# Edge weights and one-hot numbers read from PSUM in a graph attention kernel

## The chip, the cores and the metric

One core of one Trainium2 chip. The metric is the time of one execution in microseconds of device time; lower is better. The core has five engines that run beside each other: TensorE (PE in the profile), VectorE (DVE), ScalarE (ACT), GpSimd (POOL) and SyncE (SP), which here only issues transfers. They tell each other through semaphores what is done.

## What is computed

A layer norm with ReLU, and two graph attention layers with four heads of 64 channels over 12,500 nodes and 200,000 edges that are sorted by their destination, plus a self loop for each node. Cut to what matters:

```python
def _gat_layer(h_in, W, a_s, a_d, b, src, dst, n):
    h = (h_in @ W).reshape(n, Hh, Cc)
    alpha_s = jnp.sum(h * a_s, axis=-1)
    alpha_d = jnp.sum(h * a_d, axis=-1)
    e = jax.nn.leaky_relu(alpha_s[src] + alpha_d[dst], 0.2)
    m = jax.lax.stop_gradient(jax.ops.segment_max(e, dst, num_segments=n))
    ex = jnp.exp(e - m[dst])
    alpha = ex / jax.ops.segment_sum(ex, dst, num_segments=n)[dst]
    out = jax.ops.segment_sum(h[src] * alpha[:, :, None], dst, num_segments=n)
    return out.reshape(n, Hh * Cc) + b

h = jnp.maximum(_layernorm(x), 0.0)
h = gelu(_gat_layer(h, W0, a_src0, a_dst0, b0, src, dst, n))
h = gelu(_gat_layer(h, W1, a_src1, a_dst1, b1, src, dst, n))
return x + h
```

## The kernel before

A prelude of some 200 us norms the nodes, multiplies them by W0 and stores for each node a row of 264 float32 numbers in a table in DRAM: for each of four heads 64 channels and the two logits. Then each layer is a loop over 112 steps. A step takes a chunk of 1792 edges (14 slots of 128 partitions) and a window of 128 destination nodes. For it,

- SP loads the edges' fields (`edge`, line 354), a broadcast row of destinations (`dst_b`, line 359), marks (`mark`, line 363) and the window's own rows (`self_row`, line 377). These loads are issued in this order, each behind a wait for its buffer. The load of `self_row` waits for `own_part` of four steps back, and the next step's `edge` load stands behind it in SP's order.
- POOL gathers the source rows of the edges with 14 indirect DMAs of 128 rows each (line 495) into `rows_all[u]`, one of four buffers. The group of 14 waits for the sum of four steps back and for the edge fields to land.
- DVE builds one-hots that map edges to nodes (`onehotT`, line 838, from 16-bit numbers; `onehot`, line 883, float32, 1792 elements for each partition), finds the maximum along each run of edges of one destination by scans (lines 875, 877 within a partition; 897, 899 across partitions, after PE has transposed the ends of the partitions, lines 1110 and 1111), gets the carries back through PE (lines 1117, 1118) and reads them in line 957 (`reach`), and ends with `fall`, the logit minus its maximum (line 973).
- ACT takes the exponential (line 593) and writes it straight into column 64 of each head of the gathered rows in SBUF.
- In the next body DVE multiplies the rows of slots 0 to 9 by that column in three products (line 861, parts of 4, 3 and 3 slots, so 1024, 768 and 768 elements), after a small product in line 858; ACT multiplies slots 10 to 13 with 16 small instructions (line 566). PE sums all rows by node with the one-hots (line 1128), in four parts.
- Then follow the shares of the window's own node and of the sum handed over from the window before, the mean, Gelu, and either the row for the next layer's table or the residual.

A body of the loop works on four steps at once: `after` (the newest: one-hots, scans, exponential), `now` (weighing and summing), `before` (shares and means) and `earlier` (next layer's row or residual). The loops are unrolled by four bodies. Each engine runs through its own list in a fixed order. For the DVE it is, in `dve_body`: one-hots of nodes and logits (after), product part 0 (now), residual (earlier), copy of the gathered logits to `value` (`take_values`, line 867, which waits for all 14 gathers), product part 1, the scans, product part 2, the one-hot of edges, `run_max` (line 890), scans across partitions (after), shares (before), logits and falls (after), means (before). For PE, in `pe_body`: logits to edges (line 1101), sum part 0, transposes of the ends (lines 1110, 1111), part 1, next row, part 2, carries back (1117, 1118), part 3, hand over (1138).

PSUM banks: 0 logits of edges, 1 ends of runs, 2 carries, 3 and 4 sums, 5 hand over, 6 and 7 the next layer's row. The functions that the change touches:

## Time and profile before

| | us |
|---|---|
| median of three runs | 5451.78 |
| lowest and highest | 5431.81, 5456.39 |
| the profiled execution, its own time | 5461.54 |
| its span, first to last instruction | 5459.7 |
| DVE busy | 3275.1 |
| POOL busy | 3349.7 |

The profile is of one execution. A busy time is the sum of an engine's instruction times; a line of the costliest groups gives an engine, an operation, what it writes and reads with its size, how often, the busy time and the mean of one in ns, and behind the second bar the idle time of the engine just before it and what ended most of that. "issue" there is time for which the profile shows no releaser; "remote" is an event of another engine that can't be named. A semaphore's message can come later than the end of the instruction that sent it. The ends of matmuls are modelled.

### The profile page before, as it was taken

To read this page: it belongs to the slowest core of one execution; us is meant where nothing else is said; L and a number is where in the kernel's file an instruction comes from. 1 tells how busy PE (TensorE), PEld (TensorE's weight loads), DVE (VectorE), ACT (ScalarE), POOL (GpSimd) and SP (SyncE) were. 2 spreads that over 40 slices of the span, in tenths; PEclk is the share of its full clock that TensorE was granted. 3 is DMA by queue.
4 is the path that set the end of the run, shared out by engine and by line. 5 is a ranking of instruction groups with operands and counts; after the bars stand their busy time and mean duration, and the time that the engine had idled before them with its cause. 6 is when DMAs were issued, how large, how long until landed. Compare 5 with 4: busy or idle time off the path is not lost. (4 is left out here: it accounts for less than half of the span.)

```text
span 5459.7 us, 66711 instructions
## 1 busy us (share of the span) xinstructions
PE 2814.1 (52%) x12030; PEld 2001.2 (37%) x12030; DVE 3275.1 (60%) x12165; ACT 2232.4 (41%) x6943; POOL 3349.7 (61%) x3188
## 2 busy tenths in 40 slices
PE   6454555555545555555544545455545545454544
PEld 5333433333433433333333333333333333332333
DVE  5465666555756665656645656666666655665665
ACT  4243444444434443444433334344433434343434
POOL 2466666666666666666646656666656666566563
PEclk9777777777777777767766777767767777776777
DMA  6444444444444443444434444444444444444443
GB/s 209 122 114 112 119 118 116 117 116 118 118 119 111 120 116 111 113 114 119 118 88 120 120 118 131 126 125 131 127 125 131 126 125 132 123 130 123 123 128 85
DMA packets 342321, 662.86 MB, mean 121 GB/s; under 512 B 99106, under 2 KB 211530, under 8 KB 341914
## 3 DMA queue, kind: packets, MB, share of 16 engines
q0 software_dynamic: 151056, 429.17, 29.8%
q1 hardware_dynamic: 128952, 172.16, 10.6%
q10 hardware_dynamic: 62018, 59.05, 3.2%
q14 instruction: 286, 2.34, 0.1%
q8 instruction: 9, 0.15, 0.0%
HBM read 597.44 MB, written 62.65 MB: 121 GB/s over the span
## 5 line engine op out<-in xcount | busy, mean ns | idle before, releaser
L495 POOL DMA_INDIRECT rows_all<-table,edge x3136 | 3309.3, 1055 | 2042.6 <-issue 1430.9
L1128 PE MATMUL bank<-rows_all,onehot 128*128 128x264 f32 x6272 | 2144.3, 500 | 199.8 <-remote 99.9
L1128 PEld LDWEIGHTS bank<-rows_all,onehot 128*128 128x128 f32 x6272 | 1513.7, 252 | 569.1 <-issue 244.1
L566 ACT ACTIVATE rows_all<-rows_all 128x64 f32<-128x64 f32 x3584 | 877.2, 333 | 10.3 <-issue 6.8
L1101 PE MATMUL bank<-logit_p,onehotT 128*128 128x24 bf16 x3136 | 118.7, 180 | 1209.8 <-issue 875.7
L861 DVE TENSOR_TENSOR rows_all<-rows_all 128x768 f32<-128x768 f32 (+1 forms) x672 | 695.1, 1035 | 0.0
L1101 PEld LDWEIGHTS bank<-logit_p,onehotT 128*128 128x128 bf16 x3136 | 101.4, 103 | 1315.3 <-issue 1160.8
L897 DVE TENSOR_TENSOR_SCAN runs<-mark,runs,bank 4x128 f32<-4x128 f32 x224 | 104.8, 468 | 733.2 <-issue 635.3
L579 ACT ACTIVATE share<-node_d 128x8 f32<-128x8 f32 x224 | 46.7, 209 | 1162.1 <-DVE node_d L944 809.8
L602 ACT ACT_TABLE_LOAD x224 | 287.4, 1283 | 567.7 <-issue 409.5
L883 DVE TENSOR_TENSOR onehot<-iota_f,dloc 128x1792 f32<-128x1792 f32 x224 | 453.7, 2026 | 1.8 <-remote 0.9
L1138 PE MATMUL bank<-total,heir 128*128 128x264 f32 x448 | 182.8, 496 | 489.0 <-DVE heir L979 251.6
L579 ACT ACT_TABLE_LOAD x222 | 284.8, 1283 | 163.3 <-issue 160.6
L574 ACT ACTIVATE act_oT<-bank 128x256 f32<-128x256 f32 x112 | 42.5, 379 | 643.8 <-remote 531.3
L1138 PEld LDWEIGHTS bank<-total,heir 128*128 128x128 f32 x448 | 79.2, 221 | 591.4 <-DVE total L978 333.1
L593 ACT ACTIVATE rows_all<-fall 128x56 f32<-128x56 f32 x224 | 67.8, 303 | 511.3 <-DVE fall L973 315.7
L957 DVE TENSOR_TENSOR reach<-edge,bank 128x112 f32<-128x112 f32 x224 | 59.8, 267 | 339.5 <-remote 300.6
L1117 PE MATMUL bank<-ident,carry 4*128 4x4 f32 x224 | 49.3, 220 | 397.1 <-DVE carry L904 310.3
L588 ACT ACTIVATE own_part<-self_row,share 128x64 f32<-128x64 f32 x896 | 239.2, 357 | 0.0
L1154 PE MATMUL bank<-w_ext,act_oT 128*128 128x264 f32 x448 | 138.4, 437 | 171.3 <-issue 121.7
L584 ACT ACTIVATE old_part<-bank,share 128x65 f32<-128x65 f32 x896 | 208.2, 316 | 9.6
L1117 PEld LDWEIGHTS bank<-ident,carry 4*128 4x128 f32 x224 | 32.5, 145 | 482.2 <-issue 482.2
(163 smaller groups left out, 3545.5 us busy)
## 6 DMA issues: line engine op xcount, KB each, us to landing
dst_b<-dst_row SPq DMA_DIRECT2D x224, 448.0 KB
rows_all<-table,edge POOLq DMA_INDIRECT x3136
self_row<-table SPq DMA_DIRECT2D x224, 132.0 KB
table<-row ACTq DMA_DIRECT2D x113, 132.0 KB
x_row<-in_x_dram SPq DMA_DIRECT2D x112, 128.0 KB
out_dram<-y_out ACTq DMA_DIRECT2D x112, 128.0 KB
act_pad<-act_o ACTq DMA_DIRECT2D x112, 128.0 KB
table<-row ACTq DMA_DIRECT2D x24, 528.0 KB, 3.8
```

The lines of the kernel that those rows point to most:

```text
L495: nc.gpsimd.indirect_dma_start(out=G[u][:, j, :], out_offset=None, in_=table[L][0:N, :], in_offset=bass.IndirectOffsetOnAxis(ap=index[:, j ...
L566: last = nc.scalar.activation(G4[t.u][:, j, h, 0:C], G4[t.u][:, j, h, 0:C], ACT.Copy, scale=G4[t.u][:, j, h, C:C + 1])
L579: nc.scalar.activation(share[:], node_d[:], ACT.Exp).then_inc(s["share_ready"], 1)
L584: last = nc.scalar.activation(old_part[:, h, :], bank[5][:, h * HW:h * HW + C + 1], ACT.Copy, scale=share[:, 1, h:h + 1])
L588: last = nc.scalar.activation(own_part[:, h, :], self_row[t.u][:, h * HW:h * HW + C], ACT.Copy, scale=share[:, 0, h:h + 1])
L602: nc.scalar.activation(act_o[t.half][:], mean_o[:], ACT.Gelu).then_inc(s["act_ready"], 1)
L861: nc.vector.tensor_tensor(rows[:, :, 0:C], rows[:, :, 0:C], rows[:, :, C:C + 1].broadcast_to([P, (t1 - t0) * H, C]), ALU.mult).then_inc(s[ ...
L883: nc.vector.tensor_tensor(onehot[t.half][:], wide(iota_f[:], 1, SLOTS), wide(dloc[:], 2, P), ALU.is_equal).then_inc(s["onehot_ready"], 1)
L1101: last = nc.tensor.matmul(bank[0][:, j * w:(j + 1) * w], onehotT[t.half][:, j, :], logit_p[:].rearrange("d q k h -> d (q k h)"), start=Tru ...
L1128: last = nc.tensor.matmul(bank[3 + t.half][:, 0:ROW], onehot[t.half][:, j, :], G[t.u][:, j, :], start=(j == 0), stop=(j == SLOTS - 1))
L1138: nc.tensor.matmul(bank[5][:, 0:ROW], heir[:], total[:].rearrange("p h c -> p (h c)"), start=True, stop=True).then_inc(s["old_done"], 1)
L1154: last = nc.tensor.matmul(bank[7][:, 0:ROW], act_oT[:, j, :], w_ext[:, 1, j, :], start=(j == 0), stop=(j == KC - 1))
```

## The change

Three things:

1. The exponentials of an edge chunk are written to PSUM (`edge_w`, bank 2) and then copied from there by ACT into the rows' column in SBUF. The DVE's three products and the small product in front of them take the weight from `edge_w`; ACT's own products and PE's sum still use the column.
2. The numbers 0 to 127 with which the one-hot of edges is compared lie in PSUM (`numbers`, bank 1) instead of in SBUF (`iota_f`). The carries move from bank 2 to bank 1 (`carries`). As PE and DVE now both use bank 1, PE's transposes of the ends also wait for the one-hot of the same step and for `reach` of the step before.
3. The one-hot of edges goes from behind the third product to a place in front of `take_values`, which waits for the gathered rows.

```diff
+        numbers = bank[1][:, 2 * P:3 * P]
+        carries = bank[1][:, 3 * P:3 * P + 2 * H]
+        edge_w = bank[2][:, 0:SLOTS * H]
...
             def weigh_last(t):
-                act.wait_ge(s["w_ready"], t.done(0))
+                act.wait_ge(s["wcol_ready"], t.done(0))
...
             def exponentials(t):
                 act.wait_ge(s["fall_ready"], t.done(0))
-                nc.scalar.activation(G4[t.u][:, :, :, C].rearrange("p t h -> p h t"), fall[:], ACT.Exp).then_inc(s["w_ready"], 1)
+                nc.scalar.activation(edge_w.rearrange("p (t h) -> p h t", h=H), fall[:], ACT.Exp).then_inc(s["w_ready"], 1)
+                act.wait_ge(s["w_ready"], t.done(0))
+                nc.scalar.activation(G4[t.u][:, :, :, C], edge_w.rearrange("p (t h) -> p t h", h=H), ACT.Copy).then_inc(s["wcol_ready"], 1)
...
+            dve.wait_ge(hnT_copied[0], GROUPS * GROUP // 2 + 1 + 1)
+            nc.vector.tensor_copy(numbers, iota_f[:]).then_inc(numbers_ready, 1)
+            dve.wait_ge(numbers_ready, 1)
...
                 if part == 0:
-                    dve.wait_ge(s["w_ready"], t.done(0))
-                    nc.vector.tensor_tensor(G4[t.u][:, :, :, C + 1].rearrange("p t h -> p h t"), G4[t.u][:, :, :, C].rearrange("p t h -> p h t"),
+                    dve.wait_ge(s["wcol_ready"], t.done(0))
+                    nc.vector.tensor_tensor(G4[t.u][:, :, :, C + 1].rearrange("p t h -> p h t"), edge_w.rearrange("p (t h) -> p h t", h=H),
                                             value[:, 1, :, 0:SLOTS], ALU.mult).then_inc(s["wmax_ready"], 1)
                 rows = G[t.u][:, t0:t1, :].rearrange("p t (h c) -> p (t h) c", h=H)
-                nc.vector.tensor_tensor(rows[:, :, 0:C], rows[:, :, 0:C], rows[:, :, C:C + 1].broadcast_to([P, (t1 - t0) * H, C]), ALU.mult
+                nc.vector.tensor_tensor(rows[:, :, 0:C], rows[:, :, 0:C], wide(edge_w[:, t0 * H:t1 * H], 2, C), ALU.mult
                                         ).then_inc(s["weighted"][part], 1)
...
-                nc.vector.tensor_tensor(onehot[t.half][:], wide(iota_f[:], 1, SLOTS), wide(dloc[:], 2, P), ALU.is_equal
+                nc.vector.tensor_tensor(onehot[t.half][:], wide(numbers, 1, SLOTS), wide(dloc[:], 2, P), ALU.is_equal
...
                 if after:
+                    one_hots_of_edges(after)
                     take_values(after)
...
                 if after:
-                    one_hots_of_edges(after)
                     run_maxima(after)
...
             def ends_to_rows(t):
...
+                pe.wait_ge(s["reach_ready"], t.done(1))
+                pe.wait_ge(s["onehot_ready"], t.done(0))
...
-                nc.tensor.transpose(bank[2][:, 0:H], carry[:, 0, :], ident[0:H, 0:H])
-                nc.tensor.transpose(bank[2][:, H:2 * H], carry[:, 1, :], ident[0:H, 0:H]).then_inc(s["carryT_done"], 1)
+                nc.tensor.transpose(carries[:, 0:H], carry[:, 0, :], ident[0:H, 0:H])
+                nc.tensor.transpose(carries[:, H:2 * H], carry[:, 1, :], ident[0:H, 0:H]).then_inc(s["carryT_done"], 1)
...
                     pe.wait_ge(s["wmax_ready"], t.done(0))
+                    pe.wait_ge(s["wcol_ready"], t.done(0))
```

## Rows read from the trace of the kernel before

**Rows 1.** The page, busy time, share of the span and instructions by engine.
```profile
PE 2814.1 (52%) x12030; PEld 2001.2 (37%) x12030; DVE 3275.1 (60%) x12165; ACT 2232.4 (41%) x6943; POOL 3349.7 (61%) x3188
```
**Rows 2.** Line 495, the gathers: min/median/max ns, first and last start, who waited.
```profile
L495 POOL DMA_INDIRECT rows_all<-table,edge x3136: 940/946/3469, 182.3 to 5404.2; - x196
...
  DVE value L867: 50.5, 4
```
**Rows 3.** The page, costliest groups: busy us, mean ns | idle before, releaser.
```profile
L495 POOL DMA_INDIRECT rows_all<-table,edge x3136 | 3309.3, 1055 | 2042.6 <-issue 1430.9
...
L861 DVE TENSOR_TENSOR rows_all<-rows_all 128x768 f32<-128x768 f32 (+1 forms) x672 | 695.1, 1035 | 0.0
L897 DVE TENSOR_TENSOR_SCAN runs<-mark,runs,bank 4x128 f32<-4x128 f32 x224 | 104.8, 468 | 733.2 <-issue 635.3
...
L883 DVE TENSOR_TENSOR onehot<-iota_f,dloc 128x1792 f32<-128x1792 f32 x224 | 453.7, 2026 | 1.8 <-remote 0.9
...
L957 DVE TENSOR_TENSOR reach<-edge,bank 128x112 f32<-128x112 f32 x224 | 59.8, 267 | 339.5 <-remote 300.6
```
**Rows 4.** Timeline of all engines, 1500 to 1550: start us, us, what [idle before].
```profile
1510.39 0.20 PE L1118 MATMUL bank<-ident,carry 4*128 4x4 f32 x1
...
1525.53 0.27 DVE L957 TENSOR_TENSOR reach<-edge,bank 128x112 f32<-128x112 f32 x1 [13.24 <-remote]
...
1530.85 0.26 DVE L858 TENSOR_TENSOR rows_all<-rows_all,value 128x56 f32<-128x56 f32 x1
...
1534.34 2.02 DVE L883 TENSOR_TENSOR onehot<-iota_f,dloc 128x1792 f32<-128x1792 f32 x1
1534.64 2.68 POOL L495 DMA_INDIRECT rows_all<-table,edge  x1 [0.30 <-issue]
```
**Rows 5.** Timeline of POOL, the first gather of each of seven groups in a row.
```profile
1504.85 0.94 POOL L495 DMA_INDIRECT rows_all<-table,edge  x1 [0.30 <-issue]
...
1528.13 0.95 POOL L495 DMA_INDIRECT rows_all<-table,edge  x1 [6.09 <-DMA edge<-edges]
...
1552.52 0.94 POOL L495 DMA_INDIRECT rows_all<-table,edge  x1 [5.14 <-DMA edge<-edges]
...
1575.10 0.94 POOL L495 DMA_INDIRECT rows_all<-table,edge  x1 [5.10 <-DMA edge<-edges]
...
1597.48 0.94 POOL L495 DMA_INDIRECT rows_all<-table,edge  x1 [2.76 <-issue]
...
1618.28 0.95 POOL L495 DMA_INDIRECT rows_all<-table,edge  x1 [0.30 <-issue]
...
1641.68 0.99 POOL L495 DMA_INDIRECT rows_all<-table,edge  x1 [6.21 <-DMA edge<-edges]
```
**Rows 6.** Timeline of SP's transfers, 1498 to 1552: the edge loads.
```profile
1525.49 0.34 SPq L354 DMA_DIRECT2D edge<-edges  x1
...
1549.90 0.34 SPq L354 DMA_DIRECT2D edge<-edges  x1
```
**Rows 7.** Timelines of DVE and then of PE, 1606 to 1625.
```profile
1610.16 0.28 DVE L875 TENSOR_TENSOR_SCAN ahead<-turn,value 128x60 f32<-128x60 f32 x1 [0.29 <-DVE value L867]
...
1620.55 0.47 DVE L897 TENSOR_TENSOR_SCAN runs<-mark,runs,bank 4x128 f32<-4x128 f32 x1 [7.01 <-issue]
...
1612.84 0.27 PE L1111 MATMUL bank<-ident,behind 128*4 128x128 f32 x1
```
**Rows 8.** More groups of the DVE by line and shape, columns as in rows 3.
```profile
L838 DVE TENSOR_SCALAR onehotT<-dst_b,node 128x1792 bf16<-128x1792 int16 x224 | 155.3, 693 | 62.8 <-remote 37.4 <-issue 18.8 <-DVE node L829 4.0
...
L983 DVE TENSOR_TENSOR summed<-total,own_part 128x256 f32<-128x256 f32 x224 | 93.8, 419 | 1.3 <-ACT own_part L588 1.3
L978 DVE TENSOR_TENSOR total<-old_part,bank 128x260 f32<-128x260 f32 x224 | 93.7, 418 | 8.8 <-ACT old_part L584 8.8
...
L967 DVE TENSOR_TENSOR pre<-value,of_node 128x112 f32<-128x112 f32 x224 | 61.9, 276 | 7.6
```
**Rows 9.** Timeline of ACT, 1525 to 1537: the exponential.
```profile
1527.20 0.30 ACT L593 ACTIVATE rows_all<-fall 128x56 f32<-128x56 f32 x1 [13.45 <-DVE fall L973]
```

More of the change, by code:

```diff
@@ L209, in two_layer_graph_attention @@
         stores_begun, carries_begun = sem("stores_begun"), sem("carries_begun")
-        zero_stored = sem("zero_stored")
+        zero_stored, numbers_ready = sem("zero_stored"), sem("numbers_ready")
         tail_landed, tail_ready, tail_stored = sem("tail_landed"), sem("tail_ready"), sem("tail_stored")
@@ L230, in two_layer_graph_attention @@
                      "carryT_done of_node_ready known_ready reach_ready reached_ready max_ready pre_ready logit_ready fall_ready "
-                     "w_ready wmax_ready act_weighted sum_done weight1_ready weightr_ready mmax_ready absent_ready emax_ready total_max_ready "
+                     "w_ready wcol_ready wmax_ready act_weighted sum_done weight1_ready weightr_ready mmax_ready absent_ready emax_ready total_max_ready "
                      "self_z_ready old_z_ready max_z_ready node_l_ready node_d_ready no_old_ready old_max_ready least_max_ready share_ready old_part_ready own_part_ready "
@@ L957, in falls @@
                 nc.vector.tensor_tensor(reach[:], wide(edge[t.u][:, E_FIRST:E_LAST + 1, :], 2, H),
-                                        wide(bank[2][:, 0:2 * H].rearrange("p (k h) -> p k h", k=2), 3, SLOTS), ALU.add
+                                        wide(carries.rearrange("p (k h) -> p k h", k=2), 3, SLOTS), ALU.add
                                         ).then_inc(s["reach_ready"], 1)
```

## The prediction

> **What bounds the kernel now.** I read the page first. Of the engines GpSimd (POOL) is busiest with 61% and VectorE (DVE) second with 60%; TensorE has 52%, ScalarE 41% [rows 1]. No engine is full, so the question is what the loop waits for. Steps follow each other at (5404.2 - 182.3) / 224 = 23.3 us, from the first and last of the 3136 gathers, 14 a step [rows 2]. The line table says what fills them: POOL issues the gathers and stands idle for 2042.6 us around them; the DVE has four large instructions a step, three products in line 861 and the compare of line 883 [rows 3]. A gather takes 946 ns in the median but 1055 ns in the mean, with a longest of 3469 ns [rows 2, 3]: something stretches some of them. The timeline shows what. The gather that starts at 1534.64, during the one-hot compare of line 883 (1534.34 to 1536.36), takes 2.68 us instead of 0.95 [rows 4]. So a group of 14 gathers lasts 17.2 us undisturbed and up to 20.5 us otherwise [rows 5].
>
> Then I read what stands between two groups, because a shorter group is worth only what this idle time doesn't take back. The rows give the start of seven groups in a row and the idle time in front of each; so from first start to last end (next start less idle time less start) six groups last 17.2, 19.2, 17.5, 19.6, 20.5 and 17.2 us; the idle time behind them is 6.1, 5.1, 5.1, 2.8, 0.3 and 6.2 us; together 23.3, 24.4, 22.6, 22.4, 20.8 and 23.4 us [rows 5]. The next group waits for its edge load. SP issued that load 3.4 us after the end of the first group and 2.5 us after the end of the second, and it took 2.6 us from there to the first gather [rows 5, 6]. SP and PE both look slow while the later gathers of a group run, and quick again just behind it: the carry transposes of line 1118 ended at 1510.6, but the DVE's line 957, which waits for nothing else, began at 1525.53, 15 us later, within 0.1 us of SP's edge load and 3.5 us after the group of gathers had ended [rows 4 to 6]. The same happens in front of line 897, which waits for the transposes of line 1111: these ended at 1613.1, and line 897 began at 1620.55, with 7.0 us of idle time before it [rows 7]. In total the DVE stands 733.2 us in front of line 897 and 339.5 us in front of line 957 [rows 3]. What slows these messages isn't in the trace; that it goes with the gathers is. The kernel is thus bound by POOL's groups and by what can only go on when a group has passed; PE and ScalarE are not the bound.
>
> **Part 1: weights and numbers from PSUM.** The three products of line 861 and the compare of line 883 now read one operand from PSUM and one from SBUF, instead of two from SBUF. I take this to free the gathers. What is lost to stretching is 3136 x (1055 - 946) ns = 342 us [rows 2, 3]. Of the large DVE work that can do it, 695.1 us (line 861) and 453.7 us (line 883) change, and 155.3 us (line 838, a compare of 16-bit numbers) stays [rows 3, 8], so 1149 / 1304 = 88% of 342 us, or 301 us, goes: 1.34 us a step. Bounds: none of it, if the place of the operand isn't what blocks; 342 us, if all. I take 301.
> The four instructions themselves: none of this form is in the trace of before. The nearest rows are 260 elements with one operand from PSUM (line 978, 418 ns) beside 256 from SBUF alone (line 983, 419 ns), and 112 elements with one from PSUM (line 957, 267 ns) beside 112 from SBUF (line 967, 276 ns) [rows 3, 8]. So between -10 and +5 ns each, and I take nothing.
> One rule of the Trainium skill speaks against that. VectorE: DVE Perf Modes, section "The TRN2 errata", gives a fixed cost of 58 cycles with SBUF and 120 with PSUM; by it the four would cost 62 / 0.96 = 65 ns more each, an estimate of 58 us of DVE time over 224 steps. Lines 978 and 983 don't bear it out.
> A second rule bears on the core of the change. SBUF — State Buffer, section "Who interferes with whom", says that a VectorE instruction with two SBUF inputs contends with a GpSimd instruction that reads SBUF, but infers that tensor_tensor leaves descriptor generation alone, since that needs the write side. By the inference this part would be worth 0 us. The gather of 2.68 us beside the compare speaks for contention.
>
> **How much of the 301 us arrives.** Where SP's edge load comes only behind the group (four of the six boundaries, idle of 5 to 6 us), the load follows the group's end forward and the gain is whole. Where idle time is 2.8 us, SP was partly ahead; with the group 2.2 us shorter the same SP is late and perhaps a third is left. Where it is 0.3 us (one of six), the gain is whole if the load had landed over 2 us early, else little. And the three disturbed groups average 22.5 us with their idle time, the three undisturbed 23.1 us: so in part a long group only uses idle time that would be there anyway. Between whole and nothing I take 0.6: 180 us.
>
> **Part 2: the one-hot goes in front of the copy of the values.** The DVE does the same work in another order. The wait for the rows that it now precedes stood for 50.5 us in the whole run, four times [rows 2]; at most that is gained, and I take 0. The scans of lines 875 and 877 come 2.0 us later, behind the compare, while line 897 keeps its place: products and compare stand in front of it either way. So PE has 2.0 us less to do its transposes in. In the one step both can be read in, the first scan began at 1610.16 and took 0.28 us, the second is as long, and PE, which does the first part of the sum before, did its second transpose at 1612.84 [rows 7]; scans 2.0 us later would have been just in time. The cover is that part of the sum; without it the step would lose up to 2.0 us, 448 us in all. I take 0.1 us a step, 20 us. The compare also needs the sum of two steps back, some 3 us earlier than now; that sum ends in the body before and I take 0. PE's transposes now wait for the compare too, which the order of the DVE gives for nothing, and for the reach of the step before, long done.
>
> **Part 3: exponentials into PSUM, then a copy.** ScalarE gets 224 copies of 128x56, by the nearest row 0.30 us, the exponential of the same size [rows 9], so 67 us of busy time. The product of line 858 waits for it: the exponential started at 1527.20 and took 0.30 us, the copy would end near 1527.9, and line 858 began at 1530.85 [rows 4, 9]. 3 us of other DVE work cover it. Behind it on ScalarE stand the row copy, its store, Gelu and the 16 products of line 566, each 0.35 us later. Only the last of PE's four parts of the sum needs those products, so they have the three other parts as cover. I take 0. If the cover were gone: 224 x 0.35 = 78 us.
>
> **Part 4: the rest.** The carries move to another bank: nothing. One copy of 128x128 and a wait in the prelude: under 0.5 us, by the 419 ns of 256 elements in line 983 [rows 8]. PE gets one or two more wait instructions a step: 224 x 0.05 = 11 us at most.
>
> **Sum.** 5459.7 - 180 + 20 = 5300 us by the span of the profiled execution; its own time was 5461.5 and the median of the three runs 5451.8, so 10 us off: 5290 us.
>
> **Rivals.**
> A. The gain arrives whole: 5452 - 301 = 5150 us. For it: POOL is the busiest engine, and all that hangs on the end of a group moves with it. Against it: the boundaries of 2.8 and 0.3 us.
> B. The gain goes into idle time: the DVE and SP need their 22 to 23 us between two groups whatever POOL does, and the idle time grows by what the gathers lose. 5440 us, between 5400 and 5470. For it: groups of 17.2 us have 6 us behind them, that of 20.5 us has 0.3. The same time comes out if the place of the operand doesn't matter and gathers stay at 1055 ns; the rows of POOL would tell the two apart.
> C. Slower: the transposes of line 1111 come later within the group of gathers, and more often into its slow part, so that line 897 stalls until the group has passed. The stall read above was 7.0 us, and all of them sum to 733.2 us, 3.3 us a step [rows 3, 7]. At 26 more such stalls (of 224 steps) 180 us eat up the gain; at 40 more, 280 - 180 puts it at 5550 us, at 50 at 5620 us. For it: PE's transposes lose their 2 us of slack, and faster gathers bring the slow part forward. Against it: line 897 itself isn't later.
>
> **Chances.** The forecast (part of the gain) 0.43, 5200 to 5370 us; A 0.2, 5110 to 5200 us; B 0.19, 5400 to 5470 us; C 0.18, above 5480 us. The trace has the stretching beyond doubt; what it leaves open is the idle time. The range leaves out C and a bit of A: 5120 to 5480 us. A measurement of this kernel can tell about 0.5%, 27 us, from no change. Faster by more: forecast and A, with a fourth of B, 0.68; within: 0.14; slower: 0.18.
>
> **What would show it.** Gathers of about 960 ns in the mean, none of 2 us or more beside line 883, prove part 1. A median of 946 and a mean of 1055 ns as before would mean that the operand's place isn't the cause. Idle time of POOL over 2042.6 us by 100 or more shows B's mechanism, and how much of the gain it took. Idle time in front of line 897 well above 733 us is C. Products at 1035 ns in the mean and the compare at 2026 ns [rows 3] would prove that PSUM costs nothing. (65 ns more would be the figure of the Trainium skill's page.) An idle time in front of line 858 would show the copy on the path.

## The result, and the profile after

The changed kernel took 5709.3 us (median; 5695.3 to 5726.0) against 5454.1 us (5431.8 to 5507.1) for the kernel before on the same chip: a ratio of 1.0438, 95% interval 1.0381 to 1.0495. It is 4.4% slower. The prediction said 5290 us, faster.

One plain fact is needed to understand every later number. The kernel before takes 5432 to 5496 us in some measurements and 4523 to 4528 us in others, with nothing in between. (These are medians; single executions lie between 5432 and 5507 us, or between 4513 and 4528 us.) The first kind shows what the prediction had read: SP's instructions and PE's messages are held up while a group of gathers runs. I call that **the held condition** and the other **the free condition**. It doesn't seem to belong to a chip: the chip that the record numbers 15 gave 5496 us (beside i1) and, 13 minutes later, 4528 us (beside k2). The first measurement was made in the held condition. In the free condition the same change is 6.7% faster (0.9335, interval 0.9320 to 0.9351).

The page of the changed kernel in the held condition, busy time and then costliest groups (busy us, mean ns | idle before, releaser); these lines answer to [rows 1, 3]:

```profile
PE 2991.2 (52%) x12030; PEld 2085.2 (36%) x12030; DVE 3244.7 (57%) x12166; ACT 2270.4 (40%) x7167; POOL 3044.2 (53%) x3188
...
L499 POOL DMA_INDIRECT rows_all<-table,edge x3136 | 3003.7, 958 | 2606.4 <-issue 1567.0
...
L908 DVE TENSOR_TENSOR_SCAN runs<-mark,runs,bank 4x128 f32<-4x128 f32 x224 | 104.9, 468 | 1103.5 <-issue 1027.4
L872 DVE TENSOR_TENSOR rows_all<-rows_all,bank 128x768 f32<-128x768 f32 (+1 forms) x672 | 691.6, 1030 | 0.0
...
L894 DVE TENSOR_TENSOR onehot<-bank,dloc 128x1792 f32<-128x1792 f32 x224 | 452.0, 2018 | 0.0
...
L968 DVE TENSOR_TENSOR reach<-edge,bank 128x112 f32<-128x112 f32 x224 | 60.0, 268 | 670.0 <-remote 596.9
```

(Lines moved: 495 is now 499, 861 is 872, 883 is 894, 897 is 908, 957 is 968, 1110 and 1111 are 1124 and 1125, 1117 and 1118 are 1131 and 1132.) The gathers lost their stretching, 1055 to 958 ns in the mean, 305.6 us in all, as Part 1 said. But POOL's idle time grew from 2042.6 to 2606.4 us, 564 us. The DVE's idle time in front of line 908 grew from 733.2 to 1103.5 us and in front of line 968 from 339.5 to 670.0 us, 701 us together. PSUM cost the products and the compare nothing: 1035 to 1030 ns and 2026 to 2018 ns [rows 3].

The timeline of all engines, 3974 to 3990, shows one stall from its beginning to its end:

```profile
3974.90 2.02 DVE L894 TENSOR_TENSOR onehot<-bank,dloc 128x1792 f32<-128x1792 f32 x1
3975.08 0.95 POOL L499 DMA_INDIRECT rows_all<-table,edge  x1 [0.30 <-issue]
...
3978.47 0.27 PE L1125 MATMUL bank<-ident,behind 128*4 128x128 f32 x1
...
3980.96 0.70 SPq L381 DMA_DIRECT2D self_row<-table  x1
...
3982.61 0.95 POOL L499 DMA_INDIRECT rows_all<-table,edge  x1 [0.30 <-issue]
3986.15 0.47 DVE L908 TENSOR_TENSOR_SCAN runs<-mark,runs,bank 4x128 f32<-4x128 f32 x1 [6.92 <-issue]
3986.50 0.33 SPq L358 DMA_DIRECT2D edge<-edges  x1
...
3989.05 0.95 POOL L499 DMA_INDIRECT rows_all<-table,edge  x1 [5.49 <-issue]
```

The compare no longer stretches the gather beside it (0.95 us; it was 2.68 us in [rows 4]). The transposes end at 3978.7. Line 908 also waits for SP's load of the marks, but that had been issued over 40 us before the scan in every stall, so it isn't what came last (worked out from the traces). Yet line 908 starts at 3986.15, 2.6 us behind the end of the last gather (3983.56), and SP's edge load goes off 0.35 us after it. So here the DVE and SP are let go together when the group has passed, and the next group can only begin at 3989.05. Over the whole run the edge load went off behind the end of the former group in 212 of 223 cases, in the median 3.3 us behind it; in the kernel before it was 156 cases and 1.8 us (worked out from the two traces).

How often: I counted, for each step, how many gathers of the running group had begun when the second transpose ended, and whether line 897 (908) began over 2 us later (worked out from the traces, held condition; "k1" and "l1" are the experiments below).

| second transpose ends | before | changed | Part 1 alone (i1) | with a pause (k1) | edge load first (l1) |
|---|---|---|---|---|---|
| behind 1 to 5 gathers: steps, held | 66, 4 | 61, 8 | 57, 8 | 59, 5 | 35, 7 |
| behind 6 to 8 | 17, 8 | 34, 27 | 48, 35 | 8, 0 | 63, 62 |
| behind 9 to 14 | 94, 77 | 120, 120 | 109, 109 | 120, 100 | 109, 109 |
| between two groups | 47, 1 | 9, 0 | 10, 0 | 37, 1 | 17, 0 |
| held, of 224 | 90 | 155 | 152 | 106 | 178 |

The count is a little rough: a scan can begin 2 us late because the DVE is busy. By idle stretches over 2 us in front of the scan the last row reads 84, 155, 154, 105 and 178.

Two things changed at once. The part of a group in which a message is held begins earlier: before, 9 of 19 messages sent behind 9 gathers were held and 18 of 19 behind 10; in the changed kernel it was 7 of 14 behind 5 and 13 of 17 behind 6 (counted in the same way). And the message seldom falls between two groups any more (9 steps, not 47).

### The profile page after: what moved, and what is told of

It is laid out like the page before. It is cut to its first block and busy times, and to the rows that moved or that the text cites. A ratio compares the mean times of both kernels' runs of the same rounds, so it can differ in the third digit from the quotient of the medians.

```text
span 5716.0 us, 67191 instructions
## 1 busy us (share of the span) xinstructions
PE 2991.2 (52%) x12030; PEld 2085.2 (36%) x12030; DVE 3244.7 (57%) x12166; ACT 2270.4 (40%) x7167; POOL 3044.2 (53%) x3188
## 5 line engine op out<-in xcount | busy, mean ns | idle before, releaser
L499 POOL DMA_INDIRECT rows_all<-table,edge x3136 | 3003.7, 958 | 2606.4 <-issue 1567.0
L1143 PE MATMUL bank<-rows_all,onehot 128*128 128x264 f32 x6272 | 2270.2, 524 | 116.7 <-DVE rows_all L872 65.8
L1143 PEld LDWEIGHTS bank<-rows_all,onehot 128*128 128x128 f32 x6272 | 1588.3, 264 | 519.3 <-issue 163.7
L908 DVE TENSOR_TENSOR_SCAN runs<-mark,runs,bank 4x128 f32<-4x128 f32 x224 | 104.9, 468 | 1103.5 <-issue 1027.4
L872 DVE TENSOR_TENSOR rows_all<-rows_all,bank 128x768 f32<-128x768 f32 (+1 forms) x672 | 691.6, 1030 | 0.0
L1153 PE MATMUL bank<-total,heir 128*128 128x264 f32 x448 | 227.0, 602 | 793.4 <-DVE total L989 510.8
L894 DVE TENSOR_TENSOR onehot<-bank,dloc 128x1792 f32<-128x1792 f32 x224 | 452.0, 2018 | 0.0
L1153 PEld LDWEIGHTS bank<-total,heir 128*128 128x128 f32 x448 | 96.8, 269 | 915.2 <-DVE total L989 720.6
L598 ACT ACTIVATE bank<-fall 128x56 f32<-128x56 f32 x224 | 49.5, 221 | 850.8 <-DVE fall L984 688.1
L849 DVE TENSOR_SCALAR onehotT<-dst_b,node 128x1792 bf16<-128x1792 int16 x224 | 157.9, 705 | 93.3 <-issue 45.9
L1001 DVE SCALAR_TENSOR_TENSOR mean_o<-summed,inv,bias 128x64 f32<-128x64 f32 x896 | 196.0, 281 | 25.8 <-remote 15.6
```

Source lines behind the costliest of these rows:

```text
L499: nc.gpsimd.indirect_dma_start(out=G[u][:, j, :], out_offset=None, in_=table[L][0:N, :], in_offset=bass.IndirectOffsetOnAxis(ap=index[:, j ...
L872: nc.vector.tensor_tensor(rows[:, :, 0:C], rows[:, :, 0:C], wide(edge_w[:, t0 * H:t1 * H], 2, C), ALU.mult).then_inc(s["weighted"][part], 1)
L894: nc.vector.tensor_tensor(onehot[t.half][:], wide(numbers, 1, SLOTS), wide(dloc[:], 2, P), ALU.is_equal).then_inc(s["onehot_ready"], 1)
L1001: last = nc.vector.scalar_tensor_tensor(out=mean_o[:, h * C:(h + 1) * C], in0=summed[:, h, :], scalar=inv[:, h:h + 1], in1=bias[:, t.L, h ...
L1143: last = nc.tensor.matmul(bank[3 + t.half][:, 0:ROW], onehot[t.half][:, j, :], G[t.u][:, j, :], start=(j == 0), stop=(j == SLOTS - 1))
L1153: nc.tensor.matmul(bank[5][:, 0:ROW], heir[:], total[:].rearrange("p h c -> p (h c)"), start=True, stop=True).then_inc(s["old_done"], 1)
```

## The experiments

All runs, in the order of the measurements; "before" is the kernel before on the same chip beside them.

| run | what it is | us | before | condition |
|---|---|---|---|---|
| e1_psum_only | Part 1 (and 3) alone | 4218.4 | 4522.7 | free |
| e2_order_only | Part 2 alone | 4527.4 | 4522.7 | free |
| e3_after_paused | the change, with a pause on POOL | 4483.9 | 4522.7 | free |
| e4_scans_first | Part 1, scans ahead of the products | 4235.0 | 4522.7 | free |
| f1_before_again | before, for its profile | 4525.8 | 4524.5 | free |
| f2_after_again | the changed kernel | 4222.8 | 4524.5 | free |
| g1_after_storm | the change, 240 extra messages a step from SP | 4812.0 | 4523.5 | free |
| h1_weights_only | only the weights from PSUM | 4473.4 | 4523.5 | free |
| h2_numbers_only | only the compare's numbers from PSUM | 4375.2 | 4523.5 | free |
| i1_psum_only_late | as e1 | 5701.3 | 5495.8 | held |
| j1_paused_late | as e3 | 4485.8 | 4523.6 | free |
| j2_weights_late | as h1 | 4471.7 | 4523.6 | free |
| j3_order_late | as e2 | 4527.0 | 4523.6 | free |
| j4_scans_late | as e4 | 4235.8 | 4523.6 | free |
| k1_paused_third | as e3 | 5469.5 | 5439.3 | held |
| k2_scans_third | as e4 | 4243.0 | 4528.5 | free |
| k3_scans_fourth | as e4 | 5598.1 | 5432.5 | held |
| l1_edge_early | the change, SP's edge load ahead | 5665.1 | 5463.6 | held |

The expectations of the first four were built on a kernel before of about 5450 us, so their absolute figures could not be met once it ran 4523 us; what they tell apart is read from the differences. f1 and f2 were made to see what had changed.

**Part 1 alone, and Part 2 alone.** e1 puts the compare back behind the third product (and keeps its numbers in bank 2, since PE would otherwise wait for it); e2 is the kernel before with the compare moved. The edit shown is that of e1; e2's is the opposite move.

```diff
                 if after:
-                    one_hots_of_edges(after)
                     take_values(after)
...
                 if after:
+                    one_hots_of_edges(after)
                     run_maxima(after)
```

> The changed kernel with the one-hot of edges back in its old place behind the third product; the numbers lie in bank 2, so that PE's transposes need not wait for the one-hot. Weights and numbers still come from PSUM. In the changed kernel every message of PE that is sent after the sixth gather of a group arrives only when the group is over. Theory P (the place): the move of the one-hot puts the transposes of the ends 2 us later and so into that stretch; then this kernel gains what was forecast, 5200 to 5400 us, and the idle time in front of the scans across partitions is at or under the 733 us of before. Theory R (the rate): it is the undisturbed gathers, which reach the sixth 1 to 2 us earlier, that bring the stretch forward; then this kernel is slower than before as well, 5550 to 5750 us, with 950 us or more of idle time there, while a gather takes 958 ns. Theory X (the exponential's detour over PSUM is on the path): 5550 or more, with idle time in front of the small product.

> The kernel before with the one-hot of edges moved in front of the copy of the values, and nothing else: all operands from SBUF, gathers at 1055 ns. Theory P: slower than before by most of what the change costs, 5600 to 5700 us, idle time in front of the scans across partitions over 950 us. Theory R: within 1% of before, 5400 to 5510 us, since the gathers are still stretched. If both have a share, in between.

Measured: e1 0.9326 (0.9310 to 0.9342), 304 us less than before; e2 1.0008 (0.9998 to 1.0017), 5 us more. The moved compare costs at most some 5 us: 5 us without Part 1, with an interval that takes in no change, and 4 us with it (4222.8 against 4218.4 us, on two chips). In the free condition the whole of the change's effect is thus Part 1's.

**The kernel before and the changed one, again.**

> The kernel before, unchanged, for its trace. In the four runs just made the kernel before took 4522 us instead of 5454, and no engine waited for messages of PE: gathers followed gathers with 0.5 us of idle time between groups. If that difference is a property of the chip or its state and not of the kernel, this trace has either of two forms: groups of 18.9 us with 0.5 us between them and 4520 us in all, or 4.5 us between them, SP's instructions stretched to 0.7 us, and 5450 us.

> The changed kernel, unchanged. Where messages are not held up, POOL's groups alone set the time: 224 x (17.6 - 18.9) = -290 us against the kernel before, so a ratio of 0.93 to 0.94, about 4230 us beside 4522. Where they are held up as in the first measurement, 1.04 again. A ratio between them, or 1.04 without held messages, would say that the cause of the loss isn't the held messages.

Measured: 4524.5 and 4222.8 us, 301.7 us less; the working of Part 1 gave 301. First POOL in the page of before (free condition), then in that of the changed kernel, columns as above:

```profile
L495 POOL DMA_INDIRECT rows_all<-table,edge x3136 | 3306.6, 1054 | 1122.3 <-issue 1120.5
```

```profile
L499 POOL DMA_INDIRECT rows_all<-table,edge x3136 | 3008.4, 959 | 1120.8 <-issue 1113.8
```

The busy times are those of the held condition ([rows 3]: 3309.3). The idle time is what differs: 1122 us, made up of the 0.30 us between two gathers of a group (2912 x 0.30 = 874), 0.48 us between two groups (107 us) and 128 us ahead of the first group. A group and its gap last 18.7 + 0.5 = 19.2 us before and 17.4 + 0.5 = 17.9 us after. Here POOL is the bound, and what the gathers lose is what the kernel gains. The DVE now waits for rows: in front of `value` 798.6 us before and 379.2 us after. PE's message isn't late: the update came 14 ns behind the end of the transpose in the median (worked out from the trace), and line 908 stood idle 4.4 us in the whole run, against 1103.5 us.

The answers for SP's line 381, first of the changed kernel in the held condition, then in the free one (min/median/max ns):

```profile
L381 SPq MOVE self_row<-table x224: 3/700/1393, 178.6 to 5659.3; - x112
L381 SPq DMA_DIRECT2D self_row<-table x224: 3/699/729, 178.7 to 5660.7; - x112
```

```profile
L381 SPq MOVE self_row<-table x224: 29/29/37, 178.6 to 4163.9; - x112
L381 SPq DMA_DIRECT2D self_row<-table x224: 332/342/898, 178.7 to 4164.0; - x112
```

The instruction MOVE of this line, which in the free condition takes 29 to 37 ns, reads 700 ns in the median and up to 1393. That speaks for SP itself being held there, and not only its queue. But this line stands in the late part of most groups: over all of SP's MOVEs the median is 29 ns in both conditions (worked out from the traces). And the shortest reads 3 ns, far under the 29 of the free condition. So times of SP in a held stretch can't be taken as the lengths of its instructions; whether the instruction or its record was late, these rows don't tell.

**Which operand does it.** h1 takes the numbers from SBUF again, h2 the weights.

```diff
-                nc.vector.tensor_tensor(onehot[t.half][:], wide(numbers, 1, SLOTS), ...
+                nc.vector.tensor_tensor(onehot[t.half][:], wide(iota_f[:], 1, SLOTS), ...
...
-                nc.vector.tensor_tensor(rows[:, :, 0:C], rows[:, :, 0:C], wide(edge_w[:, t0 * H:t1 * H], 2, C), ALU.mult
+                nc.vector.tensor_tensor(rows[:, :, 0:C], rows[:, :, 0:C], rows[:, :, C:C + 1].broadcast_to(...), ALU.mult
```

> The changed kernel with the numbers of the one-hot read from SBUF again; the three products still take the weight from PSUM. Where messages aren't held, POOL's groups set the time, so this tells how the 301 us divide. By busy time (products 695 us, compare 454 us, 60 to 40) it gains 180 us and the other part 120. By length it is the other way round: a gather that starts under the 2.0 us compare can be held longer than one under a product of 1 us, so this one gains only 90 to 130 us (ratio 0.971 to 0.980). If only one of the two mattered, 0 or 301 us.

> The changed kernel in which the three products take the weight from the column in SBUF again; only the compare reads PSUM. By busy time it gains 120 us, by length 170 to 210 us (ratio 0.954 to 0.962). The two runs' gains should sum to about 301 us if each gather is held by one instruction alone.

Measured: h1 0.9891 (0.9874 to 0.9907), 50 us less than before, gathers 1040 ns; h2 0.9679 (0.9663 to 0.9695), 148 us less, gathers 1006 ns. POOL's busy time of line 499 (495) falls by as much: from 3306.6 to 3260.0 and to 3153.9 us. Both gains are under those forecast by length (90 to 130 and 170 to 210 us), and they don't follow busy time either (180 and 120 us). The gains alone sum to 198 us, the two forms together to 302. So these two instructions stretch gathers when both inputs lie in SBUF, the compare more than the products, though its busy time is less. In the free condition I took the gathers that lasted over 60 ns more than the median of 946 ns, and put the excess of each down to the DVE instruction that overlapped it most. In the kernel before the excess is 192 us beside the compare and 96 us beside the products; in h1, where only the compare still has two SBUF inputs, it is 245 us beside the compare (worked out from the traces). That fits a gather which is no longer delayed by the one and then meets the other, but no run shows it step by step.

**The change, as slow on POOL as before.** A memset behind the fifth gather fills the group up again, on POOL alone; all else of the change stays.

```diff
+                        pool.wait_ge(s["pause_done"], t.done(1))
...
+                            if j == 4:
+                                nc.gpsimd.memset(pause[:], 0.0).then_inc(s["pause_done"], 1)
```

> The changed kernel, in which POOL fills a buffer that nobody reads after the fifth gather of each group; the fill takes about 1.3 us, so a group lasts about 19 us again, as before, though no gather is stretched. Theory R: the stretch in which messages wait opens later, and the kernel gets faster by making POOL slower: 5400 to 5600 us. Theory P: groups are 1.5 us longer and nothing is won: 5709 us or up to 330 us more.

Measured in the free condition: 4483.9 us, 261 us more than the changed kernel. Line 501 of its page, the gathers, and line 505, the pause:

```profile
L501 POOL DMA_INDIRECT rows_all<-table,edge x3136 | 3012.0, 960 | 1091.3 <-issue 1053.1
...
L505 POOL MEMSET pause<- 128x1400 f32 x224 | 287.3, 1283 | 0.1
```

The group grows from 17.39 to 18.55 us, 224 x 1.16 = 260 us. Here POOL's time goes to the end one for one.

**Are too many messages the cause?** g1 lets SP send 240 more in each step.

```diff
+                        for n in range(240):
+                            nc.sync.sem_inc(storm[n % 4], 1)
```

> The changed kernel in which SP sends 240 more semaphore increments a step, behind its load of the marks, nothing waits for them. In the first measurement PE's messages were held and two thirds of the recorded messages were missing (29,800 records against 87,300). Theory L (the load of messages): what held them is a limit on messages or on their records, which the first chip met and these do not; then 53,760 more bring messages of PE that come late, POOL idle for over 1 us between groups, and a time over 4400 us. Theory C (a condition of that chip that the kernel doesn't cause): PE's messages stay as they are, and the time is 4223 us, or up to 50 us more by SP's 5 us a step.

Measured: 4812.0 us, 589 us more than the changed kernel, and a miss of the expected size, for 240 increments hold SP for some 14 us a step (58 ns each). But no message is held: PE's messages came 13 to 14 ns behind their matmuls in the median, as in the other free runs. The time comes from SP's loads going out late: POOL's idle time grew by 592 us (1120.8 to 1712.7), and the DVE waits for the own rows, as this line of its page says:

```profile
L860 DVE CAST logit_p<-self_row 128x8 bf16<-128x8 f32 x224 | 40.0, 179 | 998.6 <-DMA self_row<-table 998.6
```

So in the free condition this many more messages of SP (53,760 in all) don't bring on held ones.

**Part 1 alone, in the held condition.** This is the kernel of e1, met by chance in the held condition.

> Part 1 alone, a second time, in search of a chip that holds the messages up as in the first measurement (before at about 5450 us there, 4523 us on the others). If before takes about 4523 us here too, this kernel gives 4218 us again and the question of order against rate stays open. If before takes about 5450 us here: the theory that the shorter group alone turns the gain into a loss gives about 5700 us, as the changed kernel had; the theory that the moved one-hots are to blame gives less than before, 5450 - 301 = 5150 us at best.

Measured: 5701.3 us against 5495.8, ratio 1.0387 (1.0295 to 1.0479). The moved compare isn't needed for the loss: without it the stalls are nearly the same, as two lines of its page show.

```profile
L908 DVE TENSOR_TENSOR_SCAN runs<-mark,runs,bank 4x128 f32<-4x128 f32 x224 | 104.9, 468 | 1061.6 <-issue 997.0
...
L968 DVE TENSOR_TENSOR reach<-edge,bank 128x112 f32<-128x112 f32 x224 | 59.9, 268 | 672.2 <-remote 642.1
```

**The paused kernel, in the held condition.** Is it the shorter group, or something else that Part 1 brings (the read of PSUM, the copy, PE's extra wait)?

> The changed kernel with the pause of 1.28 us on GpSimd, a third time, wanted on a chip that holds the messages up. There: 5400 to 5520 us, as before, if the length of the group alone turns the gain into a loss; 5700 us or more if something else in the change does. On the other kind of chip 4484 us again, which tells nothing new.

Measured: 5469.5 us against 5439.3, one run of each, so the 30 us between them can't be told from nothing. The pause makes the kernel 6% slower than the changed one in the free condition and takes nearly all of the loss away in the held one. The lines of its page for POOL and for line 912 (908 in the changed kernel):

```profile
L501 POOL DMA_INDIRECT rows_all<-table,edge x3136 | 3001.2, 957 | 2074.5 <-issue 1122.1
...
L912 DVE TENSOR_TENSOR_SCAN runs<-mark,runs,bank 4x128 f32<-4x128 f32 x224 | 104.8, 468 | 837.3 <-issue 836.0
...
L972 DVE TENSOR_TENSOR reach<-edge,bank 128x112 f32<-128x112 f32 x224 | 60.0, 268 | 624.9 <-remote 610.1
```

POOL's idle time is back at 2075 us ([rows 3]: 2042.6) and the stall in front of the scan at 837 us. In the table above, no message sent behind 6 to 8 gathers is held any more (0 of 8, not 27 of 34), and 37 fall between groups. So a group as long as before takes the loss away, with everything else of the change in place. How is only in part clear: the stall in front of line 972 (968) stays at 624.9 us, so of the 701 us by which the change had lengthened the two stalls, 311 go. The DVE's other waits are 650 us, where the kernel before had 1110, and its busy time is 109 us longer than in the changed kernel. The pause stands between the fifth and sixth gather; with it the holding starts some four or five gathers later (12 of 27 messages behind 10 gathers, 51 of 55 behind 11). That looks like something that fills while gathers are issued and drains in pauses, but no run shows what it is.

**Scans ahead of the products.** e4 has Part 1's reads, the copy of the values and both scans ahead of all products, PE's transposes ahead of the first part of the sum, and the compare last.

> The changed kernel with the copy of the values and the scans within partitions in front of all three products, and PE's transposes of the ends in front of the first part of the sum; the one-hot is last, the numbers lie in bank 2. The transposes then leave some 4 us earlier in the body, before the sixth gather of most groups. By P and R alike the message gets through: 5150 to 5400 us, idle time in front of the scans across partitions under 500 us, and the stall moves to line reach. Theory X: 5650 us or more, as in the changed kernel.

> The maxima's scan before all products, once more wanted on a chip that holds the messages up (before at about 5450 us). There: 5200 to 5400 us if the loss comes from the message of PE's transposes falling into the later part of a group; 5700 us, as the changed kernel, if it doesn't hang on that message. On the other kind of chip 4240 us again.

Measured: 4235.0 us in the free condition (0.9359, 0.9343 to 0.9375), 12 us behind the changed kernel. In the held condition 5598.1 us against 5432.5, between the two figures expected. Its page:

```profile
L968 DVE TENSOR_TENSOR reach<-edge,bank 128x112 f32<-128x112 f32 x224 | 59.9, 268 | 986.9 <-remote 918.5
L908 DVE TENSOR_TENSOR_SCAN runs<-mark,runs,bank 4x128 f32<-4x128 f32 x224 | 104.6, 467 | 757.2 <-issue 757.2
```

The DVE indeed stands less in front of the scan, 757 us against 1103.5, if not the "under 500" expected. The other message, of the carries, which comes next from PE, took the stall over, as e4's expectation said: 986.9 us against 670.0. Together 1744 us and 1773 us. The loss hangs on no single message; the step needs several within one group, and most of those that fall behind the sixth gather wait.

**The edge load ahead of the own rows.** In the changed kernel POOL waited 1029.5 us for its edge load. l1 issues the next step's edge load before this step's `self_row`. The expectation names the loads of the destinations and marks too, but by the edit these stay behind it, and the fourth step of each unrolled body keeps the old order; in the trace the edge load went first in 168 of 223 cases.

```diff
                     for u in range(NB):
...
+                        if u:
+                            own_row(*waiting)
...
-                        sp.wait_ge(s["own_part_ready"], t.done(4))
-                        nc.sync.sem_inc(loads_begun, 1)
-                        sp.dma_start(self_row[u][:], table[L][bass.ds(base, P), :]).then_inc(s["self_landed"][u], 16)
+                        waiting = (t, base)
+                    own_row(*waiting)
```

> The changed kernel with SP's loads in another order: the next step's edge load (and those for its destinations and marks) ahead of this step's load of the own rows. Where messages are held up (before at about 5450 us): if the loss comes from the edge load waiting in SP's queue behind the load of the own rows, 5300 to 5500 us; if it comes from PE's messages to the DVE alone, 5700 us as the changed kernel. On the other kind of chip POOL waits only 0.48 us between groups, so nothing is to be gained: 4223 us, or a little more if the own rows come later.

Measured: 5665.1 us against 5463.6, one run of each. The wait for the edge load was halved, and the kernel is still 202 us slower than the one before. The answer for its gathers (line 507), who POOL waited for:

```profile
  DMA edge<-edges: 530.5, 53
  PE bank L1151: 345.5, 41
```

POOL now waits for the sum that frees its buffer (line 1151, 345.5 us), and the scan in front of which the DVE stands (line 916 here) waits 1282.9 us. So the place behind `self_row` in SP's order isn't what makes the loss. SP itself stays late: 147 of the 223 edge loads still went off behind the end of the former group.

**Repeats that met the free condition.** They were meant for the held one and show only that the free one repeats.

> The changed kernel with a pause of 1.28 us on GpSimd in each group, which makes the group as long as before. Wanted is a chip that holds the messages up (before at about 5470 us). If there the length of the group alone turns the gain into a loss, this kernel comes back to the time of before, 5400 to 5520 us; if it is something else in the change, it stays at the changed kernel's 5700 us or more. If before takes 4523 us on this chip, it is 4484 us again and tells nothing new.

> Weights alone from PSUM: gathers of 1040 ns in place of 1055, a group 0.2 to 0.3 us shorter. On a chip that holds the messages up: if the loss grows with the shortening of the group, about a sixth of the loss, 5470 + 40 = 5510 us; if it comes whole with the first PSUM read, 5700 us; if the order is to blame, no loss at all, 5450 us or less. On the other kind of chip 4473 us again.

> The one-hots moved in front of the wait for the rows, nothing read from PSUM. On a chip that holds the messages up: if the length of the group is what counts, within 30 us of before; if the moved one-hots bring the loss, 5650 us or more. On the other kind of chip 4527 us again.

> Both PSUM reads, and the maxima's scan before all products, so that PE's transposes go off 3 us earlier in the group of gathers. On a chip that holds the messages up: if the stall comes because the message of the transposes now falls into the later part of a group, this order takes it out again and gives less than before, 5200 to 5400 us; if the order doesn't matter, 5700 us as the changed kernel. On the other kind of chip 4235 us again.

> Both PSUM reads, with the maxima's scan before all products, a third kernel wanted on a chip that holds the messages up (before at about 5450 us). There: 5200 to 5400 us if the loss comes from the message of PE's transposes falling into the later part of a group, since they go off 3 us earlier here; 5700 us, as the changed kernel, if it doesn't hang on that message. On the other kind of chip 4236 us again, which tells nothing new.

Measured: ratios of 0.9915, 0.9886, 1.0008 and 0.9362, each within 0.0005 of the first run of its kernel; k2 4243.0 us against 4528.5. So how the loss grows with the shortening of the group (j2), and what the order alone does to the old kernel (j3), stay untried in the held condition.

No version is best in both conditions: e1 (4218.4 us) and the changed kernel (4222.8) are both at the floor that POOL's 14 gathers a step set, and in the held condition the kernel before is the fastest of those that were run.

## Why the prediction was wrong

**What bounds the kernel.** Half right. The prediction saw that SP and PE are slow behind the first gathers of a group, and that two waits of the DVE end only with it. It took that for a property of this kernel. It is a condition, and 930 us of the 5454 hang on it (5454 less 4524). No row of the profile of before could have told this, but three told that something was wrong that no instruction explained: 15 us from the end of a transpose to its reader [rows 4], and releasers named "issue" and "remote" for most of the idle time of lines 897 and 957 [rows 3]. Its page has one more sign. It gives no time to landing for SP's loads, while the page of the same kernel in the free condition does; held first, then free:

```profile
self_row<-table SPq DMA_DIRECT2D x224, 132.0 KB
```

```profile
self_row<-table SPq DMA_DIRECT2D x224, 132.0 KB, 2.5
```

**Part 1, 301 us.** Right in mechanism and in its total. 301.7 us arrive where POOL is the bound, the gathers went from 1055 to 958 ns (about 960 was forecast), none lasts over 1.51 us, and the four instructions cost nothing more. That the total came out so closely is in part luck: the 301 us were shared out by busy time, 60 to 40 between products and compare, and h1 and h2 show the larger share at the compare (50 and 148 us). The Trainium skill (VectorE: DVE Perf Modes, "The TRN2 errata") gives a fixed cost of 120 cycles with PSUM and 58 with SBUF. The 65 ns more that the prediction estimates from it do not appear: the compare went from 2026 to 2018 ns. The Trainium skill (SBUF — State Buffer, "Who interferes with whom") infers that tensor_tensor leaves descriptor generation alone. The gathers here don't bear that out: h2 gained 148 us from the place of one operand.

**"Between whole and nothing I take 0.6: 180 us."** This is the step that failed. The range from nothing to whole was itself wrong: nothing arrived, and the kernel lost 255 us. The reasons given for less than whole were the boundaries of 2.8 and 0.3 us, and that a long group in part only uses idle time that would be there anyway. The step did not stay at 23.3 us, it grew to 24.5, since the idle time isn't what is left over: it is set by when messages are held, and this moves with the gathers. By the DVE's account, from the held profile of before to that of after: busy time 30 us less, waits for the two PE messages 701 us more (1073 to 1773), all other waits 414 us less (1110 to 696), in all 256 us more, which is the difference of the spans (5716.0 - 5459.7). What other waits give up, the two messages took back and more. The 414 us aren't all the gain of a faster POOL: in k1, whose groups are as long as before, the other waits fell as well, to 650 us, so a longer stall at one line also takes the place of a wait at another.

**Rival A,** that the gain arrives whole, is what the free condition shows: 301.7 us. Its time of 5150 us came nowhere, since it was worked out from the held 5452.

**Rival B,** that idle time takes the gain, was right as far as it went: the idle time of POOL grew by 564 us where the mark was 100. It ended at no change, and the run went beyond.

**Rival C** was what happened, at 0.18. It named the place (line 897, now 908), the mark (idle time well above 733 us; it was 1103.5) and one of the two right causes, "faster gathers bring the slow part forward" (by some four gathers, see the counts under the table). Its other cause, that PE's transposes lose 2 us through the moved compare, isn't needed: i1 has the compare in the old place and nearly the same stall. Its price was too small: it went up to 50 more stalls, at 5620 us, and counted only one message. Counting idle stretches over 2 us in front of each line, there were 71 more at line 908 (84 to 155) and 41 more at line 968 (35 to 76).

**Part 2, +20 us.** Measured +5 us and +4 us in the free condition, neither clear of noise. In the held one the change (+255 us over its before) and Part 1 alone (+206 us, interval 163 to 263) can't be told apart.

**Part 3 and Part 4, 0.** Right. Line 869 (858 before) has 0.0 us of idle time in front of it, so the copy stayed hidden; the two lines of ScalarE in the free profile of the changed kernel:

```profile
L600 ACT ACTIVATE rows_all<-bank 128x56 f32<-128x56 f32 x224 | 61.6, 275 | 7.1
L598 ACT ACTIVATE bank<-fall 128x56 f32<-128x56 f32 x224 | 49.5, 221 | 236.9 <-DVE fall L984 229.1
```

**What stays open.** What holds the messages, and why at one time and not at another on the same chip. Shown: where it holds, a longer group by a pause takes the loss away (k1, one run); more messages from SP don't bring it on in the free condition (g1); and the kernels before and after both meet it. Not excluded is the recording of the profile itself: the times of the experiments come with a span and a granted clock read from such a record, in the held condition most of the updates are missing from it, and no time taken without one is on record. TensorE's granted clock is lower in the mean too, 0.717 before and 0.702 after where the free condition has 0.759 and 0.770, and a matmul of the sum took 524 ns in the changed kernel where it was 500. The traces fit a TensorE that stands idle longer, but its share in the loss wasn't separated. Not tried: a slower group by other means, or fewer gathers with more rows each.

## What to carry over

Where an engine waits for a message long after its sender is done, and the releaser reads "issue" or "remote", the idle time is no slack of the kernel: don't multiply a gain by a share of it, and put as much chance on a loss as on the gain. Time the kernel before on several chips or at several times before tuning against such a wait; here one change is worth -6.7% or +4.4% by that alone. And move one of two SBUF operands of a large VectorE instruction to PSUM where GpSimd issues gathers beside it: that part held in every run.

## What was not expected of the hardware

- The held condition: the same kernel takes 5432 to 5496 us or 4523 to 4528 us. In it, the MOVE of line 381 of SP reads 700 ns in the median and not 29, and a reader of PE's message began up to 31.6 us behind the matmul, with its engine idle for 30.4 us of that (line 897 of the kernel before, at 2883 us). The trace of before holds 28,459 semaphore updates there and 87,125 in the free condition; so in the held condition updates are missing from the record.
- What was held is often let go only behind the last gather of a group. In the changed kernel 190 of the 231 stalls over 2 us at lines 908 and 968 ended between two groups, in the median 2.8 us behind the last gather; in the kernel before it was 74 of 119, and 2.0 us. The others ended while gathers were running.
- A pause of 1.28 us inside each group of gathers makes the kernel 240 us faster in the held condition (5469.5 against 5709.3, measured at different times) and 261 us slower in the free one.
- One PSUM operand in place of SBUF costs the compare and the products nothing, and takes the gather beside the compare from 2.68 us to 0.95.
- An increment of a semaphore by SP took 58 ns.
